# Grouped attention on Trainium2: the rotary exchange of halves moved from VectorE to ScalarE, and the sine product to GpSimd

## The reference, cut to what matters

```python
def apply_rope(x, cos, sin):
    x1, x2 = jnp.split(x, 2, axis=-1)
    return jnp.concatenate([x1 * cos - x2 * sin, x2 * cos + x1 * sin], axis=-1)
q = apply_rope((x @ wq).reshape(b, s, 16, 128), cos, sin)
k = apply_rope((x @ wk).reshape(b, s, 4, 128), cos, sin)
scores = einsum('bqhd,bkhd->bhqk', q, repeat(k, 4)) / sqrt(128)
probs = softmax(where(causal, scores, min))
out = einsum('bhqk,bkhd->bqhd', probs, repeat(v, 4)) @ wo
```

## Time and profile before

| what | value |
|---|---|
| time before, median of 3 runs | 1097.96 us (1096.91 to 1099.07) |
| the profiled execution's own time | 1096.07 us |
| its span | 1094.3 us |
| busy PE / DVE / ACT / POOL over the span | 88% / 65% / 44% / 35% |
| the grouped attention's start to the end of its loop | about 593 to 866 us of the span |
| mean granted TensorE clock | 0.955 of full speed |

### The profile page before, as it was taken

How to read it: one execution, slowest core, us unless ns; L and a number is a source line. 1 busy time by engine, 2 the same in 40 slices (tenths; PEclk the granted TensorE clock), 3 DMA queues, 4 the chain that set the end, 5 groups by cost and what they waited for, 6 DMA issues and landing times. The chain is left out here.

```text
span 1094.3 us, 19650 instructions
## 1 busy us (share of the span) xinstructions
PE 968.1 (88%) x7073; PEld 784.4 (72%) x7083; DVE 713.4 (65%) x1324; ACT 478.8 (44%) x1082; POOL 381.1 (35%) x416
## 2 busy tenths in 40 slices
PE   9788989978999999999997898998979884999970
PEld 5455666647888888888874687886868533999970
DVE  3476768875555565665555687877878652888845
ACT  4221355534544555544443343444434422666630
POOL 2000300005666765676741344444434323000005
PEclk9899989999999999999998999999999886999995
DMA  4000100023333343343311000000000157655503
GB/s 172 1 1 1 29 1 1 1 96 104 106 109 105 97 121 98 92 118 108 94 50 44 1 26 19 19 24 19 24 0 19 59 194 253 227 210 203 203 29 115
DMA packets 55931, 87.40 MB, mean 80 GB/s; under 512 B 4784, under 2 KB 46000, under 8 KB 53680
## 3 DMA queue, kind: packets, MB, share of 16 engines
q1 hardware_dynamic: 54320, 82.19, 23.1%
q0 software_dynamic: 1536, 4.20, 1.2%
HBM read 75.36 MB, written 11.01 MB: 79 GB/s over the span
## 5 line engine op out<-in xcount | busy, mean ns | idle before, releaser
L1550 ACT ACTIVATE e_probs<-ps,e_neg_max 128x128 f32<-128x128 f32 (+1 forms) x128 | 52.8, 417 | 112.8 <-DVE e_neg_max L1497 112.8
L1106 DVE TENSOR_TENSOR d_s_m<-ps,d_decay 128x768 f32<-128x768 f32 x64 | 58.3, 952 | 51.1 <-PE ps L1269 51.1
L120 PE MATMUL ps<-xTl,d_wh 128*128 128x512 f32 x192 | 80.0, 417 | 0.0
L120 PE MATMUL ps<-xTh,d_wh 128*128 128x512 f32 x192 | 76.4, 398 | 0.0
L120 PE MATMUL ps<-xTh,d_wl 128*128 128x512 f32 x192 | 76.3, 397 | 0.0
L120 PE MATMUL ps<-wl_gated,f_wh 128*128 128x256 f32 x240 | 69.0, 288 | 3.2 <-DVE wl_gated L1849 2.0
L1189 ACT ACTIVATE d_gated_hi<-d_gated 128x512 fp32r<-128x512 f32 x32 | 20.2, 632 | 110.6 <-DVE d_gated L1112 110.6
L129 PE MATMUL ps<-warm 128*128 128x512 bf16 x221 | 59.4, 427 | 9.8 <-PEq L1364 3.2
L120 PE MATMUL ps<-wh_gated,f_wh 128*128 128x256 f32 x240 | 67.7, 282 | 0.0
L120 PE MATMUL ps<-wh_gated,f_wl 128*128 128x256 f32 x240 | 67.7, 282 | 0.0
L1783 POOL DMA_INDIRECT xT<-slot_outs,f_slots x8 | 7.7, 962 | 153.7 <-DMA slot_outs<-f_rows 151.5
(11 more groups left out here) (352 smaller groups left out, 3189.7 us busy)
## 6 DMA issues: line engine op xcount, KB each, us to landing
f_stage<-in_w_experts SPq DMA_DIRECT2D x15, 1536.0 KB, 6.7
d_decay<-in_decay SPq DMA_DIRECT2D x32, 384.0 KB, 3.7
d_stage<-in_w_decay SPq DMA_DIRECT2D x32, 256.0 KB, 3.1
d_stage<-in_w_decay SPq DMA_DIRECT2D x32, 128.5 KB, 3.6
d_stage_v<-in_w_decay SPq DMA_DIRECT2D x32, 128.0 KB, 2.3
d_stage<-in_w_decay SPq DMA_DIRECT2D x32, 128.0 KB, 2.5
slot_rows<-warm SPq DMA_DIRECT2D x1, 3840.0 KB, 12.8
slot_outs<-f_rows SPq DMA_DIRECT2D x15, 256.0 KB, 2.1
```

The lines of the kernel that those rows point to most:

```text
L120: mm = pe.matmul(out, w(k), x(k), start=(n == 0), stop=(n == 3 * len(ks) - 1))
L1106: dve.tensor_tensor(s_m[:, s % 2, 2 * b:2 * b + 2, :], ps[:, 2 + 2 * b:4 + 2 * b, 0:CAUSAL], decay[:], ALU.mult).then_inc(sm_ready, 1)
L1550: act.activation(probs[:, t % 4, cols], bank[:, cols], ACT.Exp, bias=neg_max[:, t % 4, b:b + 1], accum_out=sums[:, t % 4, b:b + 1]).then_i ...
```

## The change

The rotation is spread over three engines. DVE keeps only the cosine product. ACT, after DVE has read the bank, copies the halves crossed over from the bank to a new SBUF tile `swapped` (two instructions of 64 partitions), and this frees the bank (`swap_ready` in place of `turned_ps`). POOL multiplies `swapped` by the sine table and then subtracts the result from the cosine product. The table's signs are as they were, so the sum becomes a difference. In the start, ACT's crossed copies are put between the copies of the values.

```diff
+        swapped = sb("swapped", [P, 2, 512])
...
             else:
-                eng.wait_ge(turned_ps, projected(g, last))
+                eng.wait_ge(swap_ready, projected(g, last))
...
             def rotate(key, count, slot):
-                pool.wait_ge(turned_ps, count)
+                pool.wait_ge(swap_ready, count)
                 dst = k_T[:, half_of(key)] if key[0] == "k" else q_T[:, key[1] // 2 % 2, half_of(key)]
-                pool.tensor_tensor(dst, by_cos[:, slot, :], by_sin[:, slot, :], ALU.add).then_inc(roped, 1)
+                pool.wait_ge(roped, count - 2)
+                pool.tensor_tensor(by_sin[:, slot, :], swapped[:, slot, :], rope[:, 1 if key[0] == "k" else 3], ALU.mult).then_inc(sin_ready, 1)
+                pool.wait_ge(sin_ready, count)
+                pool.tensor_tensor(dst, by_cos[:, slot, :], by_sin[:, slot, :], ALU.subtract).then_inc(roped, 1)
...
             def rotate(key, count, slot, bank):
                 dve.wait_ge(proj_ps, count)
                 dve.wait_ge(roped, count - 2)
-                cos, sin = (rope[:, 0], rope[:, 1]) if key[0] == "k" else (rope[:, 2], rope[:, 3])
-
-                dve.tensor_tensor(by_cos[:, slot, :], bank, cos, ALU.mult)
-                dve.tensor_tensor(by_sin[0:HDQ // 2, slot, :], bank[HDQ // 2:P], sin[HDQ // 2:P], ALU.mult)
-                dve.tensor_tensor(by_sin[HDQ // 2:P, slot, :], bank[0:HDQ // 2], sin[0:HDQ // 2], ALU.mult).then_inc(turned_ps, 1)
+                dve.tensor_tensor(by_cos[:, slot, :], bank, rope[:, 0 if key[0] == "k" else 2], ALU.mult).then_inc(turned_ps, 1)
...
-            for t in range(NT):
-                act.wait_ge(v_ps, LEAD + t + 1)
-                act.activation(v_all[:, t, :], ps[:, 6 + t % 2, :], ACT.Copy).then_inc(v_ready, 1)
+
+            def swap(count, slot, bank):
+                act.wait_ge(turned_ps, count)
+                act.wait_ge(roped, count - 2)
+                act.activation(swapped[0:HDQ // 2, slot, :], bank[HDQ // 2:P], ACT.Copy)
+                act.activation(swapped[HDQ // 2:P, slot, :], bank[0:HDQ // 2], ACT.Copy).then_inc(swap_ready, 1)
+
+            for n, key in enumerate(first):
+                swap(LEAD + n + 1, n % 2, ps[:, 4 + at[key] % 2, :])
+                for t in (2 * n, 2 * n + 1):
+                    act.wait_ge(v_ps, LEAD + t + 1)
+                    act.activation(v_all[:, t, :], ps[:, 6 + t % 2, :], ACT.Copy).then_inc(v_ready, 1)
...
+                    if t in project_at:
+                        key = project_at[t]
+                        swap(projected(g, key), order.index(key) % 2, ps[:, 4 + at[key] % 2, :])
                     if t >= 2 and t in project_at:
                         u = t - 2
...
-            pe.wait_ge(turned_ps, LEAD + 2)
+            pe.wait_ge(swap_ready, LEAD + 2)
             project(first[2])
...
-            pe.wait_ge(turned_ps, LEAD + 3)
+            pe.wait_ge(swap_ready, LEAD + 3)
             project(first[3])
```

More of the change, by code:

```diff
@@ L1390, in layer1_grouped_attention @@
             ctx, "e", "w_hi w_split turned_ps nm_ready rs_ready v_copied pT_ready wo_high wo_split o_low")
-        act_sems = v_ready, p_ready, o_high = c.sems(ctx, "e", "v_ready p_ready o_high")
-        pool_sems = roped, pn_ready = c.sems(ctx, "e", "roped pn_ready")
+        act_sems = v_ready, p_ready, o_high, swap_ready = c.sems(ctx, "e", "v_ready p_ready o_high swap_ready")
+        pool_sems = roped, pn_ready, sin_ready = c.sems(ctx, "e", "roped pn_ready sin_ready")
         block = ctx.enter_context(nc.Block())
```

## The result

The changed kernel took 1140.03 us (median of 4 runs, 1136.25 to 1149.51) against 1097.46 before: a ratio of 1.040, interval 1.037 to 1.043, slower by 42.6 us. The forecast was slower, at 1128 with a range from 1109 to 1139. The direction holds, and so do the waits that the forecast is made of; the median stands 1 us above the range, because one term is missing. The four runs lie in the order of their mean granted clock: 1136.25 us at 0.949, 1139.50 and 1140.56 at 0.947, 1149.51 at 0.936.

The account below looks back on a forecast made before the run. PE was taken as the bound, busy 57.05 of 63.07 us in a group, with waits on chains deciding. Four groups at +6.9 us (27.6) plus the start's 3.7 made 31.3 on 1096.07; forecast 1128 us, range 1109 to 1139.

Parts of the forecast that it names:

- the sum: Whole kernel: 6.9 us per group, four times 27.6, plus the start's 3.7, giving 31.3 us more.
- The head: Start of each group: step 4's scores wait for POOL's rotation, chain 1.15 us longer, projection 0.15 earlier: +1.0 us.
- Steps 5 to 12: Steps 5 to 8 and 9 to 12 of each group: later maximum and longer rotation chain, +1.85 us each.
- The doubled turn: Steps 5, 9 and 16: DVE's cast and subtraction meet two POOL instructions; weights' subtraction 1.4 to 1.7 us, was 0.43.
- The walk from the maximum to the scores of step 8: Steps 5 to 8: exponentials, crossed copies and POOL's two instructions take 5.35 us instead of 4.53, 0.8 more.
- a sign of wrong steps: PE waiting for turned probabilities rather than for rotations would show the forecast's steps wrong; no size given.
- Steps 13 to the next group: Steps 13 to 15, ACT's output part behind crossed copies: +0.5 us; group's end, step 5's pattern without exponentials: +1.7.
- The start: Before the groups: projections and last rotation wait for crossed copies behind ACT's copies of values: +3.7 us in all.
- The rival in which the turns don't double: Steps 5, 9 and end: DVE's subtraction avoids POOL's second instruction; 3.1 us per group, 16 in all, 1113; chance 0.25.
- DVE's relief decides: In the groups: longer ACT and POOL chains stay hidden, PE runs at its own pace, 8.5 us faster, 1088; chance 0.08.
- POOL's queue holding up the probabilities: Normalising multiplications stand behind longer rotations on POOL; 0.5 us at five places per group adds 10 us, 1138; chance 0.12.

Follow-up runs that it names:

- e13_fill_start: Changed kernel with e11_fill_mid's zero-adding matmuls in PE's gaps and e4_start's ACT order in the start: 1128.49 us, ratio 1.028.
- e3_no_mult: Changed kernel without POOL's multiplication by the sine, POOL subtracting the crossed copy itself (rotation not fully computed): 1117.78 us, ratio 1.019.
- e2_moved: Changed kernel with the splits of output weights moved from steps 5, 9, 12, 16 to 7, 11, 12, 18: 1117.74 us, ratio 1.019.
- e5_before_moved: Kernel before, with the splits of output weights moved as in e2_moved, as a control: 1094.40 us, ratio 0.9964.
- e6_before_pool2: Kernel before, with one extra unused POOL multiplication ahead of each rotation's sum: 1129.27 us, ratio 1.029.
- e4_start: Changed kernel with ACT's start reordered, both key halves' crossed copies first and the value copies later: 1131.18 us, ratio 1.032.
- e8_all: Changed kernel with moved splits, ACT's start reordered, and the crossed copies last in ACT's step: 1129.96 us, ratio 1.029.
- e10_moved_start: Changed kernel with moved splits and ACT's start reordered, the crossed copies left in place: 1117.74 us, ratio 1.019.
- e12_before_moved2: Kernel before, with the splits of output weights at steps 7, 12, 15 and 18: 1090.72 us, ratio 0.993.
- e9_fill_trim: Changed kernel with zero-adding matmuls in PE's gaps of steps 1 to 4 and 18 only: 1136.51 us, ratio 1.037.
- e11_fill_mid: Changed kernel with zero-adding matmuls ahead of PE's waits, three at steps 7 and 11, none at 8 and 12: 1133.82 us, ratio 1.032.
- e7_act_last: Changed kernel with the loop's crossed copies moved to the end of ACT's step, behind the high part of the output: 1136.87 us, ratio 1.035.

## Why the prediction was right, and where it failed

**The step that failed** is the sum, which puts the clock at nothing without a reason. It took every duration and every step from a trace in which the groups ran at granted clock 1.00, and added waits to PE's stream as if the clock would stay. It did not: 0.91, 0.94, 0.99 and 0.98. In the profiled run this made the groups 10.7 us longer (291.7 against four times 70.25); by the medians, e13_fill_start plus the start's 4.2 us stands 7 us below the changed kernel. A term of 7 to 11 us was missing, and no rival had it. The terms that the sum does have measured 33 us (four times 7.2 in the groups, 4.3 in the start) where it has 31.3; with them alone the time would have been 1129.

**The head** (+1.0) measured +1.25. ACT's pair of crossed copies took 1.2 us, from 786.30 to 787.50, the upper bound instead of the 1.1 taken: the second starts only when the first is over. POOL's own handover is 0.08, not 0.05. e3_no_mult, without POOL's second instruction, has the head back at 12.06 us.

**Steps 5 to 12** (+1.85 twice) measured +1.75 and +2.05. The doubled turn came as forecast, and e2_moved, e5_before_moved and e6_before_pool2 show it as a cause. The walk from the maximum to the scores of step 8 (5.35 forecast, 5.54 measured from 790.43 to 795.97) had nearly the right size with an incomplete reason: I let only the rotation decide. The prediction names a PE that waits for turned probabilities rather than for rotations as a sign of wrong steps. PE does so, 1.5 us in a group against 1.1 for the rotation, and it waits 5.8 us for the high part of the output, which the prediction does not name. e3_no_mult shows ACT's order as a second path close behind it, so removing the first gains less than its price.

**Steps 13 to the next group** (+0.5 and +1.7) measured +2.2 together, but all of it at the end: 0.0 from item 12 to 15 and +2.3 behind it, where PE's longest wait for the high part of the output is 2.9 us. That the sum of the two is right is luck.

**The start** (+3.7) measured +4.3: at 602.11 and 608.45 PE waits 1.03 and 1.90 us where I had 1.2 and 1.85, and the last rotation ends at 617.43, the first scores start at 617.57. e4_start shows that ACT's order was all of it.

**The rivals.** The rival in which the turns don't double is refuted by 1.47 us. That DVE's relief decides is refuted too: e8_all and e10_moved_start, with the start's loss and the doubled turn gone, stay 20 to 32 us above the kernel before. The pace that this rival worked out for four steps, 12.98 us, did appear, but in e5_before_moved and e12_before_moved2, where DVE keeps its products and only the splits have moved. POOL's queue holding up the probabilities reached nearly the measured time with the wrong mechanism: in the changed kernel's groups no wait of PE is put down to POOL's normalised probabilities. The Trainium skill (SBUF — State Buffer, Who interferes with whom) calls the access that DVE and POOL share an exclusive lock, and says that ACT waits for nobody. These traces agree: the subtraction took 1.47 us beside POOL's instruction of 1.29, while ACT's copy at 787.91, beside POOL's product, kept its 0.38. The Trainium skill's overlap of 93 ns for back-to-back ACTIVATEs (ScalarE: Activation LUTs, What ACT_TABLE_LOAD costs) was not there for the crossed copies, which started 0.61 us apart at 0.59 each; the measurement decides.

What stays open: which groups lose the clock differs from kernel to kernel (the third lost least in the changed kernel, the first nothing in e4_start, the second nothing in e9_fill_trim), and no run here tells why.

## What to carry to other kernels

In this kernel, moving work from the busiest helper engine to idle ones bought nothing, because PE waits for a chain and not for that helper's load. So count the chain's handovers and what stands behind each new instruction on its own queue, before counting busy time. Two instructions of POOL in a row give it two turns against DVE's SBUF work, so casts and subtractions belong in steps where POOL is quiet; that alone was worth 7 us here, in the kernel before (e12_before_moved2). And when a change adds gaps to a PE stream at full clock, give the clock a term of its own in the sum.

## What the runs showed of the hardware that was not expected

- More PE work made it faster: e11_fill_mid gives PE 391 matmuls in a group instead of 349, and its median is 6 us below the changed kernel's (ratios 1.029 to 1.035 against 1.037 to 1.043), with the granted clock at 1.00 in three groups.
- In the changed kernel's groups, where PE's longest single gap was 2.9 us, the clock fell to its lower level. The same gaps did not always do it: behind heads with PE busy 8.3 of 13.3 us, the clock over items 4 to 8 was 0.90 in the changed kernel's second group and 0.92 in e7_act_last's third, and 1.00 in the changed kernel's fourth and in e7_act_last's second and fourth. The kernel before has such a head too (busy 8.08 of 12.03 us) and kept its clock.
- A cast that slips in between two POOL instructions is no gain for what follows it: at 789.04 the subtraction started 0.03 us after the cast's end and still lost the turn. The median of the weights' subtractions is 1.46 us in the changed kernel and in e6_before_pool2.
